# Causal attention on one core: the maximum pass with 96-row operands, and value visits of two key blocks

## What is computed

```
qkv = x @ w_attn.T + b_attn
scores = einsum('bhqd,bhkd->bhqk', q, k) * scale
scores = where(mask, scores, -inf)          # causal; each odd row does not see the row before it
w = softmax(scores, axis=-1)
y = einsum('bhqk,bhkd->bhqd', w, v)
return y @ w_proj.T + b_proj
```

## Time and profile before

| what | us |
|---|---|
| median of three runs | 2346.11 |
| span of the profiled execution, first to last instruction | 2324.6 |
| what the median has beside that span | 21.5 |
| first maximum pass, by itself | 33.8 |
| fifteen quads with the next quad's maximum pass | 519.72 |
| last quad, exponential pass alone | 29.72 |

### The profile page before, as it was taken

How to read it: one execution, slowest core, us unless ns; L and a number is a source line. 1 busy time by engine, 2 the same in 40 slices (tenths; PEclk the granted TensorE clock), 3 DMA queues, 4 the chain that set the end, 5 groups by cost and what they waited for, 6 DMA issues and landing times. The chain is left out here.

```text
span 2324.6 us, 36254 instructions
## 1 busy us (share of the span) xinstructions
PE 1960.7 (84%) x11363; PEld 1301.0 (56%) x11363; DVE 1764.5 (76%) x3598; ACT 958.9 (41%) x1892; POOL 907.5 (39%) x910
## 2 busy tenths in 40 slices
PE   2899997889999747989978599999999995398998
PEld 1566665756666426877866233333333363287787
DVE  7798874578887667877978577777777646687788
ACT  1222223322222443433557255555555537143345
POOL 2444442134444467887245300000000026588853
PEclk9999997989999858999989699999999996599999
DMA  5000000100000342223526534334334006222246
GB/s 177 1 0 0 0 0 14 42 0 1 0 0 0 97 159 64 92 87 101 170 69 168 98 55 70 51 54 69 50 55 70 2 1 195 75 89 89 89 148 191
DMA packets 116655, 156.59 MB, mean 67 GB/s; under 512 B 20966, under 2 KB 85772, under 8 KB 115980
## 3 DMA queue, kind: packets, MB, share of 16 engines
q1 hardware_dynamic: 99840, 112.83, 20.9%
q0 software_dynamic: 14400, 40.41, 5.6%
q10 hardware_dynamic: 2252, 1.29, 0.2%
HBM read 107.00 MB, written 47.20 MB: 66 GB/s over the span
## 5 line engine op out<-in xcount | busy, mean ns | idle before, releaser
L2021 DVE TENSOR_REDUCE t_nm<-ps 128x1 f32<-128x512 f32 (+3 forms) x768 | 390.9, 553 | 106.3 <-PE ps L2111 53.5
L2087 ACT ACTIVATE t_E<-ps 128x1024 f32<-128x1024 f32 (+3 forms) x384 | 295.0, 808 | 248.0 <-PE ps L2139 194.9
L1507 PE MATMUL ps<-m_w,m_xT 128*128 (+1 forms) x1248 | 347.1, 414 | 0.8 <-DVE m_xT L1587 0.8
L1507 PEld LDWEIGHTS ps<-m_w,m_xT 128*128 128x128 f32 x1248 | 222.5, 191 | 38.2 <-issue 1.4
L567 POOL TENSOR_TENSOR f_h<-f_h,f_hmagic 128x704 f32<-128x704 f32 x64 | 108.1, 1689 | 293.4 <-DVE f_h L209 293.4
L605 PE MATMUL ps<-wgT,f_xT 128*128 128x352 f32 x512 | 187.8, 516 | 38.5 <-DVE f_h L523 36.4
L2006 POOL COPY t_Va<-t_V 128x128 f32<-128x128 f32 x64 | 16.1, 295 | 491.7 <-DVE t_mp L2032 491.5
L2136 PE MATMUL ps<-t_Qs,t_Ks 98*128 98x512 bf16 (+3 forms) x768 | 199.8, 341 | 6.0 <-DMA t_Qs<-t_mT 4.1
L1525 PE MATMUL ps<-m_w,m_hT 128*128 (+1 forms) x1248 | 199.7, 296 | 0.5 <-DVE m_hT L1604 0.5
L639 PE MATMUL ps<-wdT,f_hT 128*128 128x256 f32 (+1 forms) x768 | 189.5, 389 | 7.4 <-DVE X L557 5.4
L1559 ACT ACTIVATE m_hT<-ps 128x256 fp32r<-128x256 f32 x208 | 80.1, 385 | 227.9 <-PE ps L1516 226.7
(11 more groups left out here) (296 smaller groups left out, 3950.0 us busy)
## 6 DMA issues: line engine op xcount, KB each, us to landing
m_raw<-in_L_ffn_rw SPq DMA_DIRECT2D x48, 256.0 KB, 3.3
t_parts<-t_qkv_part SPq DMA_DIRECT2D x64, 192.0 KB, 2.8
t_Qs<-t_parts SPq DMA_DIRECT2D x96, 128.0 KB, 4.0
t_Ks<-t_parts SPq DMA_DIRECT2D x96, 128.0 KB, 6.6
m_yl<-m_picked_out SPq DMA_DIRECT2D x40, 256.0 KB, 3.2
m_rows<-m_xn SPq DMA_DIRECT2D x16, 512.0 KB, 4.3
m_xg<-m_rows SPq DMA_DIRECT2D x64, 128.0 KB, 2.8
m_y<-m_picked_out SPq DMA_DIRECT2D x24, 256.0 KB, 3.3
```

The lines of the kernel that those rows point to most:

```text
L1507: last = nc.tensor.matmul(ps[:, H1 + u, :], xT[:, u, kx, k, :], of_expert(w1, kw, e, k), start=n == 0, stop=n == 3 * DC - 1)
L2021: nc.vector.tensor_reduce(dst, ps[:, bank, 0:n], AX_X, ALU.max, negate=True).then_inc(emptied, 1)
L2087: nc.scalar.activation(E[:, s % NPB, :, 0:n], ps[:, bank:bank + 2, 0:n], ACT.Exp, scale=float(HD) ** -0.5).then_inc(e_ok, 1)
```

## The change

Three things change. The maximum pass uses the full stacks: both heads' matmuls of a step have 96 rows of contraction and the same partitions, and `Qo`, `Ko` with their six loads per quad are gone (12 loads in place of 18). The values of two key blocks are visited together at every fourth slot from slot 7 on, the last two behind `turn_max`. For that, `E` has eight buffers in place of four, and ScalarE's copy of the first sums stands behind slot 13 in place of slot 9. The two tables are as they were.

```diff
-    LEAD = 3 * HD
-    SECOND = 64
...
-    NPB = 4
+    NPB = 8
     VW = HD + 1
-    AT_Y = 9
+    AT_Y = 13
     NQ = 3
-    ROWS_OF_QUAD = 2 * (len(QPARTS) + 3)
+    ROWS_OF_QUAD = 2 * len(QPARTS)
...
-            if i < 2 * len(QPARTS):
-                side, r = divmod(i, len(QPARTS))
-                rows = scratch[side][q:q + 1, (QPARTS, KPARTS)[side][r], :, :]
-                sp.dma_start((Qs, Ks)[side][c][r * HD:(r + 1) * HD, :, :],
-                             rows.rearrange("q (h p) t -> p (q h) t", p=HD)).then_inc(stacked[c], 16)
-                return
-            side, r = divmod(i - 2 * len(QPARTS), 3)
+            side, r = divmod(i, len(QPARTS))
             rows = scratch[side][q:q + 1, (QPARTS, KPARTS)[side][r], :, :]
-            odd = rows.rearrange("q (g o p) t -> p (q g) o t", o=2, p=HD)[:, :, 1, :]
-            sp.dma_start((Qo, Ko)[side][c][SECOND + r * HD:SECOND + (r + 1) * HD, :, :], odd).then_inc(stacked[c], 16)
+            sp.dma_start((Qs, Ks)[side][c][r * HD:(r + 1) * HD, :, :],
+                         rows.rearrange("q (h p) t -> p (q h) t", p=HD)).then_inc(stacked[c], 16)
...
-                    mine = [nc.tensor.matmul(ps[:, banks[0], 0:n], Qs[c][0:LEAD, 2 * pair, rows],
-                                             Ks[c][0:LEAD, 2 * pair, cols], start=True, stop=not diag),
-                            nc.tensor.matmul(ps[:, banks[1], 0:n], Qo[c][SECOND:SECOND + LEAD, pair, rows],
-                                             Ko[c][SECOND:SECOND + LEAD, pair, cols], start=True, stop=not diag)]
+                    mine = [nc.tensor.matmul(ps[:, bank, 0:n], Qs[c][0:STACK, 2 * pair + i, rows],
+                                             Ks[c][0:STACK, 2 * pair + i, cols], start=True, stop=not diag)
+                            for i, bank in enumerate(banks)]
...
-                        pe.wait_ge(pv_ok, q * NE + 2 * k + 6)
+                        pe.wait_ge(pv_ok, q * NE + 2 * k + 2 + NPB)
...
-                        if s % 2 and s > 1:
-                            values(q, c, (s - 3) // 2)
+                        if s % 4 == 3 and s > 3:
+                            values(q, c, (s - 7) // 2)
+                            values(q, c, (s - 5) // 2)
                     if not end:
                         turn_max(q)
+                    values(q, c, NE // 2 - 2)
                     values(q, c, NE // 2 - 1)
```

More of the change, by code:

```diff
@@ L1903, in causal_attention @@
         until_y_done = ctx.enter_context(ExitStack())
-        Qs, Ks, Qo, Ko = [], [], [], []
+        Qs, Ks = [], []
         sem = lambda s: ch.sem(name + s)
@@ L1911, in ring_of_rows @@
             Ks.append(ch.sb(f"{name}Ks{c}", [STACK + 2, QUAD, SEQ], BF16, ctx=until_y_done))
-            Qo.append(ch.sb(f"{name}Qo{c}", [SECOND + LEAD, 2, SEQ], BF16, ctx=until_y_done))
-            Ko.append(ch.sb(f"{name}Ko{c}", [SECOND + LEAD, 2, SEQ], BF16, ctx=until_y_done))
         def stack_row(sp, q, c, i):
-            if i < 2 * len(QPARTS):
-                side, r = divmod(i, len(QPARTS))
-                rows = scratch[side][q:q + 1, (QPARTS, KPARTS)[side][r], :, :]
-                sp.dma_start((Qs, Ks)[side][c][r * HD:(r + 1) * HD, :, :],
-                             rows.rearrange("q (h p) t -> p (q h) t", p=HD)).then_inc(stacked[c], 16)
-                return
-            side, r = divmod(i - 2 * len(QPARTS), 3)
+            side, r = divmod(i, len(QPARTS))
             rows = scratch[side][q:q + 1, (QPARTS, KPARTS)[side][r], :, :]
-            odd = rows.rearrange("q (g o p) t -> p (q g) o t", o=2, p=HD)[:, :, 1, :]
-            sp.dma_start((Qo, Ko)[side][c][SECOND + r * HD:SECOND + (r + 1) * HD, :, :], odd).then_inc(stacked[c], 16)
+            sp.dma_start((Qs, Ks)[side][c][r * HD:(r + 1) * HD, :, :],
+                         rows.rearrange("q (h p) t -> p (q h) t", p=HD)).then_inc(stacked[c], 16)
         def first_rows(sp, i):
@@ L2173, in _ @@
                 pe.sem_inc(y_stored, 1)
-                pe.sem_inc(pv_ok, 4)
+                pe.sem_inc(pv_ok, NPB)
                 pe.sem_inc(e_ok, 2)
```

## The result

The changed kernel takes 2382.55 us, the median of four runs (2374.49 to 2398.87), beside 2344.41 us for four runs of the kernel before (2342.00 to 2347.78). The ratio is 1.0152, with a 95% interval from 1.0109 to 1.0195: slower by 38 us by the medians (26 to 46 by the interval). The forecast was 2386, in a range from 2340 to 2408.

A forecast was written before the change was run, and what follows sets the result against it. TensorE was taken to bound the quads. Fifteen quads at +2.4 us give +36; first pass +2.8, last quad +2 and loads -0.5 make +40 on 2346: 2386 us, range 2340 to 2408.

The forecast's parts named there:

- four adjacent steps: At four places a quad a step directly follows another and waits for VectorE's first maximum: together +2.9 us.
- first two steps of a quad: TensorE already waits 0.7 us for VectorE there, so 0.2 us of the saved layout changes comes back.
- other smaller waits: Where one slot's scores lie between steps, about six times a quad, TensorE waits for maxima: bounds 0 and 1.5 us.
- a quad at full clock: Each of fifteen quads: streaming, layout changes, adjacent steps and smaller waits sum to +2.4 us.
- first maximum pass: Before the quads, at half clock, extra streams outweigh saved drains: +2.8 us, with ends -5 and +2.8.
- last quad: No steps fill gaps; three value visits move to slot 7 or later, uncovered: +2 us, ends 0 and +4.
- loads at the end of the projection: Six fewer loads a quad gain nothing in the quads, but may give back 0.5 us there.
- falls of the clock in the quads: Sum left them unchanged; a rival had new waits bring one in each quad, costing 24 us: 2410 us, chance 0.08.
- Streams and layouts: Per quad, streaming 9216 columns a second time costs +4.0 us; 49 fewer layout changes at 0.10 give -4.9.
- The waits are hidden: Rival: at adjacent steps VectorE's first maximum runs in TensorE's shadow, so faster: 2327 us, chance 0.10.
- balance: Rival: adjacent waits cost half, smaller ones nothing, +0.6 us a quad, first pass gains 5: 2350 us, chance 0.07.
- The clock stays up: Rival: longer streams keep TensorE's clock up in quads and first pass, saving 16 and 7.8 us: 2362 us, chance 0.09.

The follow-up runs named there:

- Short maxima: Changed kernel with eight extra idle-filling matmuls a quad, each VectorE maximum taken over 128 columns only; 2351.38 us, ratio 1.0018.
- full stacks only: Changed kernel with single value visits, four buffers and the copy back behind slot 9; 2342.60 us, ratio 0.9989.
- the two kept-busy kernels: Changed kernel and kernel before, each with eight extra matmuls a quad filling two TensorE idles; 2372.64 us (1.0113) and 2339.26 us (0.9974).
- double visits, kept busy: Kernel before with double value visits, eight buffers, copy behind slot 13, plus eight extra idle-filling matmuls a quad; 2391.38 us, ratio 1.0189.
- steps spread: Changed kernel with new step tables leaving one adjacent place a quad, and four extra matmuls ahead of `turn_y`; 2372.72 us, ratio 1.0109.
- double visits only: Kernel before with double value visits, eight buffers and the copy behind slot 13, keeping 48-row pairs; 2437.58 us, ratio 1.0392.

## Why the prediction was right

The sign, the mechanism and the size held, and what was measured can be set beside the terms of the sum. The 0.67 us of the second row, which the prediction has as 0.7, is this line of the kernel before:

```profile
1438.41 0.28 PE L2106 MATMUL ps<-t_Ks,t_Qs 48*128 48x256 bf16 x1 [0.67 <-DVE t_nm L2021]
```

| term, us | predicted | measured |
|---|---|---|
| four adjacent steps, a quad | 0.74, 0.76, 0.76, 0.63 | 0.75, 0.76, 0.77, 0.63 |
| first two steps of a quad, added | 0.2 | 0.15 (0.82 less 0.67) |
| other smaller waits, a quad | 0.2 | 0.41 at one place |
| full stacks with single visits, a quad | | 0.56 |
| a quad at full clock | +2.4 | +2.63 |
| fifteen quads at full clock | +36 | +39.5 |
| first maximum pass | +2.8 | +2.4 |
| last quad | +2 | +3.4 and +1.4 in the two pairs of profiles |
| loads at the end of the projection | -0.5 | not shown apart |
| falls of the clock in the quads | 0 | +3.6 and -6.5 in the two pairs |
| in all | +40 | +43 in the profiles' attention, mean of two; +38 (26 to 46) in the runs |

*The four waits* came within 0.01 us, as every piece of them (result, maximum, way back) had a row of before. *Short maxima* shows that it is VectorE's first maximum that ends them.

*Streams and layouts.* That the two nearly cancel is shown by *full stacks only*: +0.56 us, where the prediction's prices give 4.0 - 3.7 + 0.2 = 0.5 with the first two steps' share. The 0.10 us between steps and scores is gone (1574.31 to 1574.75).

*The smaller waits* were the loosest term. The four waits and the first two steps as measured, with TensorE's own -0.9 as predicted, give 2.91 + 0.15 - 0.9 = 2.16. Of the other 0.47, the place at 1572.00 has 0.41, and 0.06 is not located. The prediction had this kind of place, with one slot's scores between two steps, but as six small ones; one of them carried nearly all. The term lies within the bounds given, 0 to 1.5.

*The first pass* kept its lower clock, at which the term was chosen, and took 2.4 of 2.8 us.

*The last quad* is the weakest. With the clock up all through, as in the two kept-busy kernels, it took 28.03 us before and 31.59 changed, +3.6, near the upper end of 0 to +4; the three uncovered visits thus cost almost all of their time. In the first pair of profiles both kernels had a fall there, and the difference was 3.4; in the second only the kernel before had one (a mean clock of 0.89, beside 1.00), and it was 1.4.

*The clock.* The prediction left it as it was, and in the sum that held, by luck: each kernel lost 11 to 20 us to the half clock in its quads, and nothing in the prediction says that the two should nearly cancel. The reason it gave for pricing the rival was wrong. Falls in every quad were priced at 2.7 us each, from one quad of before (another of that trace, 1502.06 to 1539.78 us, lost 4.1), and given 0.08 because the new waits are short. They did come in every quad behind the first of one execution, and in seven of fourteen in another. A fall of the changed kernel costs only 1.3 us (37.52 - 36.22), and the kernel before lost 15.9 and 18.0 us to its own, so that 19.5 and 11.5 us in their place made little difference. Had the full stacks not been part of the change, the falls would have decided: 40.93 us a quad.

*The waits are hidden* and *balance* are out by the rows above: each adjacent step idles, in full. *The clock stays up* is out too: the first pass stayed at 0.50, and the quads lost the 19.5 and 11.5 us. *The loads* cost nothing, as held: SP's queue waits 489.3 us for the shift now, in place of 402.4. What their six fewer give back at the end of the projection no run shows apart.

## What to carry to other kernels

A table that interleaves two streams of work is written for one placing of a third: when the values move, look at what becomes adjacent, and price each such place by the other engine's hand-over, one instruction of it and the ways there and back. Slack as a sum (7 us of VectorE a quad) says nothing of that, since a single place can use only what lies beside it. And before a difference between two profiles is explained, split it by stage, and compare stages at the same granted clock: one pair of profiles here overstated the loss by 22 us.

## What the hardware showed beyond that

- The first maximum pass never left half clock, whether TensorE was busy for 17.27 us of it, for 23.10 of 34.77, or for 42.21 of 42.74. In the quads, filling one or two idles of under 1 us kept the clock up in most, not in all: three quads of *double visits, kept busy* and one of *steps spread* fell, and *full stacks only* had no fall with nothing filled. What holds it down in the pass was not settled.
- The same double visits had 13.7 us at half clock in each quad with 48-row pairs and 3.4 with 96-row operands, while the matmuls' waits were alike (3.4 and 3.3 us). The 48-row pairs alone don't make the longer stretch: kept busy, their three falls last 3.4. In *double visits only* the half clock ends about when the loads of the next quad end (the DMA share falls from 1.01 to 0.00), but *full stacks only* has loads at the same place (a share above 1.0) with no fall, so the loads alone don't explain it. One or two executions of each kernel were profiled.
- A fall can lock to the kernel's period: eleven quads in a row of 37.5 us, each with its stretch at the same place.
